# Two attentions in one kernel: algebra between them in two halves inside the loops, output per four batches inside the second loop

## The reference

```
norm_X   = layernorm(ctx, w1, b1);  norm_F = layernorm(x + tgt2, w2, b2)
attended = softmax(norm_F norm_X^T / 16) norm_X
h        = gelu(attended fc1^T + fc1_b)          # 4 values per token
cross    = h fc2^T + fc2_b                       # rank 4 plus a constant
nc       = layernorm(cross, w3, b3)
self     = softmax(nc nc^T / 16) nc
out      = norm_F + gamma2 * (cross + gamma1 * self)
```

## Time and profile before

| | us |
|---|---|
| median of 3 runs (lowest, highest) | 298.19 (297.62, 300.04) |
| the profiled execution | 298.4 |
| its span, first to last instruction | 296.5 |
| TensorE busy | 230.9 (78%) |
| VectorE busy | 203.8 (69%) |
| ScalarE busy | 138.8 (47%) |
| GpSimd busy | 115.1 (39%) |
| mean granted TensorE clock | 0.776 |
| moved by DMA | 26.79 MB, 90 GB/s mean |

### The profile page before, as it was taken

The page is one execution under the profiler, slowest core; times in us unless marked ns, Lnnn a source line. Parts: engine busy times, 40 slices in busy tenths (PEclk is TensorE's granted clock), DMA queues, the critical chain, the costliest instruction groups (busy, mean ns, idle before and its releaser), DMA issues.

```text
span 296.5 us, 4621 instructions
## 1 busy us (share of the span) xinstructions
PE 230.9 (78%) x1614; PEld 149.3 (50%) x1614; DVE 203.8 (69%) x391; ACT 138.8 (47%) x265; POOL 115.1 (39%) x141
## 2 busy tenths in 40 slices
PE   4969986199999999999999982006788888846990
PEld 4745553189888888888888850002222222212320
DVE  6586764998989888989883325994444444447991
ACT  1154572067767676767676743003533333312320
POOL 8000066979979996979972000170000000000000
PEclk9965999689999999999999999555555555555555
DMA  7940000064625262525000000000000000002997
GB/s 209 385 151 2 1 1 0 0 204 146 190 93 191 100 202 85 195 91 193 26 1 0 2 0 0 0 0 0 3 0 2 0 0 2 1 0 86 382 380 288
DMA packets 14710, 26.79 MB, mean 90 GB/s; under 512 B 1760, under 2 KB 1760, under 8 KB 14688
## 3 DMA queue, kind: packets, MB, share of 16 engines
q1 hardware_dynamic: 14688, 26.50, 25.8%
HBM read 18.11 MB, written 8.39 MB: 89 GB/s over the span
## 4 chain that ended last, share of the span: by engine, by line
PE 66%; DVE 23%; issue 4%; ACT 4%; DMA 1%; SPq 0%; DVEq 0%; ACTq 0%
PE psum L843 19%; PE psum L789 10%; DVE Fall L538 6%; PE psum L851 6%; DVE nm L493 5%; PE psum L970 5%; PE psum L812 3%; PE psum L800 3%; PE psum L940 3%; PE psum L823 3%; PE psum L881 3%; PE psum L863 3%; PE psum L759 2%; PE psum L978 1%; DVE PT L465 1%
## 5 line engine op out<-in xcount | busy, mean ns | idle before, releaser
L843 PE MATMUL psum<-XT,Fall 128*128 128x256 f32 x256 | 60.6, 379 | 0.0
L843 PEld LDWEIGHTS psum<-XT,Fall 128*128 128x128 f32 x256 | 46.1, 190 | 5.0
L575 POOL TENSOR_TENSOR xN<-xN,tgt 128x512 f32<-128x512 f32 x30 | 39.1, 1305 | 4.4 <-DVE tgt L389 2.7
L595 POOL TENSOR_SCALAR cN<-cN,nmean,rstd 128x256 f32<-128x256 f32 x64 | 36.0, 574 | 2.4 <-POOL rstd L582 2.3
L418 DVE TENSOR_REDUCE nmax<-psum 128x2 f32<-128x512 f32 x32 | 22.0, 688 | 18.7 <-PE psum L843 18.5
L692 ACT ACTIVATE PT<-psum 128x512 f32<-128x512 f32 x32 | 19.1, 597 | 33.2 <-PE psum L851 33.2
L338 DVE TENSOR_SCALAR xN<-xN,bn,rstd 128x256 f32<-128x256 f32 x64 | 29.8, 508 | 0.0
L582 POOL TENSOR_TENSOR rstd<-vps,minus_half 128x8 f32<-128x8 f32 (+1 forms) x16 | 25.3, 1580 | 9.9 <-DVE vps L329 9.7
L679 ACT ACTIVATE Fall<-psum,par 128x512 f32<-128x512 f32 x32 | 23.4, 791 | 9.2 <-PE psum L789 9.2
L698 ACT ACTIVATE E<-psum,nmax 128x256 f32<-128x256 f32 x64 | 26.6, 472 | 1.6 <-DVE nmax L418 1.6
L929 PE MATMUL psum<-identb,sU 128*128 128x128 bf16 x64 | 9.7, 306 | 19.2 <-DVE sU L273 19.2
(11 more groups left out here) (155 smaller groups left out, 369.8 us busy)
## 6 DMA issues: line engine op xcount, KB each, us to landing
cN<-ctx SPq DMA_DIRECT2D x32, 256.0 KB, 3.0
xN<-x SPq DMA_DIRECT2D x32, 256.0 KB, 4.2
out<-Fall SPq DMA_DIRECT2D x32, 256.0 KB, 3.2
x0T<-x0t SPq DMA_DIRECT2D x1, 256.0 KB, 2.7
wqT<-wqt SPq DMA_DIRECT2D x1, 256.0 KB, 3.2
c0T<-c0t SPq DMA_DIRECT2D x1, 256.0 KB, 3.8
wkT<-wkt SPq DMA_DIRECT2D x1, 256.0 KB, 4.6
wvT<-wvt SPq DMA_DIRECT2D x1, 256.0 KB, 4.9
```

What stands on the lines that cost most here:

```text
L575: pool.tensor_tensor(xN[:, b % SLOTS, :], xN[:, b % SLOTS, :], tgt2[:, :, :].rearrange("p t d -> p (t d)"), ALU.add).then_inc(y_ok, 1)
L595: pool.tensor_scalar(own, own, nmean[:, p % 4, NT * m + t:NT * m + t + 1], root_of(p, 0, m, t), ALU.add, ALU.mult)\
L843: last = pe.matmul(bank[SBANK1[b % 3]][:, t * N:(t + 1) * N], Fall[:, b, c, t * P:(t + 1) * P], XT[:, p % 4, c, m * N:(m + 1) * N], start= ...
```

## The change

- The algebra works on two groups of 32 tiles (batches 0 to 15 and 16 to 31) and is cut into six parts. Group 0's parts stand in VectorE's rounds 26 and 29 to 33 of the first loop, its GELU in ScalarE's round 28. Group 1's parts stand in steps 0 and 2 to 5 of the second loop, its GELU after the weights of step 1. GpSimd cuts group 0 before the second loop and group 1 in it.
- The products of the quadratic forms go into `kv`, the memory of the 16-head attention's keys and values, and no longer into that of `PT`.
- The transposition of the output operand (`RT`) moves from between the loops to round 30 of the first.
- The second loop has a new order on each engine. Scores have two buffers of two banks (0 to 3) in place of three; transposes of pieces and of outputs share bank 4; maxima, attended values and returns share bank 5; outputs use banks 6 and 7.
- Division and output cuts are done per quad: division on VectorE in `returned`, the cuts on GpSimd (`output_cuts`, five instructions of 8 tiles). The copy of `ha` into `co` goes to GpSimd.
- The output product comes per pair within the loop, the final addition handles two batches (1024 values per partition) per instruction, and transfers start two at a time.
- The loop has 21 steps: step `p` ends with the output of pair `p - 5`.

```diff
+GROUP = TILES // 2
+LATE = {26: (0,), 29: (1,), 30: (2,), 31: (3,), 32: (4,), 33: (5,)}
+NEXT = {0: (0,), 2: (1,), 3: (2, 3), 4: (4,), 5: (5,)}
...
-    kTm = sb("kTm", [P, 2, 2, N])
-    v1 = sb("v1", [P, NT, NH, VW])
+    kv = sb("kv", [P, 4 * N + NT * NH * VW])
+    kTm = kv[:, 0:4 * N].rearrange("p (e o n) -> p e o n", e=2, o=2)
+    v1 = kv[:, 4 * N:4 * N + NT * NH * VW].rearrange("p (t h k) -> p t h k", t=NT, h=NH)
...
-    big = PT2[:, :, :, :].rearrange("p a m n -> p (a m n)")
+    big = kv
...
     def scored(p):
-        return psum[:, 1024 * (p % 3):1024 * (p % 3 + 1)]
+        return psum[:, 1024 * (1 - p % 2):1024 * (2 - p % 2)]
+
+    def score_bank(p, m):
+        return bank[2 * (1 - p % 2) + m]
...
-            sp.wait_ge(fin_ok, b + 1)
+            sp.wait_ge(fin_ok, b // 2 + 1)
...
+        def products(v, m, n):
+
+            w = big[:, 0:GROUP * n * n].rearrange("p (t j i) -> p t j i", t=GROUP, j=n)
+            link(dve.tensor_tensor(w, v.unsqueeze(2).to_broadcast([P, GROUP, n, n]),
+                                   m.rearrange("p (j i) -> p j i", j=n).unsqueeze(1).to_broadcast([P, GROUP, n, n]),
+                                   ALU.mult))
+            return w
+
+        def newton(v, y, t):
+            link(dve.tensor_tensor(t, y, y, ALU.mult))
+            link(dve.scalar_tensor_tensor(t, t, -0.5, v, ALU.mult, ALU.mult))
+            link(dve.scalar_tensor_tensor(y, t, 1.5, y, ALU.add, ALU.mult))
+
+        def algebra(g, part):
+            G = members(g)
+            oa = OA[:, :, :, :, :].rearrange("p q t i k -> p (q t i) k")[:, G, :]
+            w5, v, y, t = W5[:, G, :], var[:, G], r3[:, G], t3[:, G]
+            if part == 0:
+                dve.wait_ge(o_saved, QUADS // 2 * (g + 1))
+                link(dve.reciprocal(rA[:, G].unsqueeze(2), oa[:, :, H:H + 1]))
+                link(dve.tensor_tensor(hpre[:, G, :], oa[:, :, 0:H], spread(rA[:, G], H), ALU.mult))
+                link(dve.tensor_tensor(hpre[:, G, :], hpre[:, G, :], c_("fc1b").unsqueeze(1).to_broadcast([P, GROUP, H]),
+                                       ALU.add), ("hpre", g))
+            elif part == 1:
+                dve.wait_ge(gelu_ok, g + 1)
+                dve.wait_ge(zero_ok, 8)
+                link(dve.tensor_reduce(w5, products(ha[:, G, :], Q[:, :], H + 1), AX.X, ALU.add))
+                link(dve.tensor_tensor(w5, w5, ha[:, G, :], ALU.mult))
+                link(dve.tensor_reduce(v, w5, AX.X, ALU.add))
+            elif part == 2:
+                link(dve.tensor_scalar(v, v, EPS, None, ALU.add))
+                link(dve.tensor_scalar(y.bitcast(I32), v.bitcast(I32), 1, None, ALU.logical_shift_right))
+                link(dve.tensor_scalar(y.bitcast(I32), y.bitcast(I32), -1.0, RSQRT_SEED, ALU.mult, ALU.add))
+                newton(v, y, t)
+            elif part == 3:
+                newton(v, y, t)
+                newton(v, y, t)
+                link(dve.tensor_tensor(u[:, G, 0:H + 1], ha[:, G, :], spread(y, H + 1), ALU.mult), ("u", g))
+            elif part == 4:
+                link(dve.tensor_reduce(uK[:, G, :], products(u[:, G, :], K[:, :], U), AX.X, ALU.add))
+            else:
+                left_cuts(uK[:, G, :], cut[:, G, 0:U], sU[:, 0, G, :], U)
+                ALG["left", g] = count[0]
...
+            for part in LATE.get(b, ()):
+                algebra(0, part)
...
         def returned(q):
+            own = slice(8 * q, 8 * (q + 1))
             dve.wait_ge(back_mm, q + 1)
-            dve.tensor_copy(OB[:, 8 * q:8 * (q + 1), :],
-                            bank[7][:, N:N + NT * P].rearrange("p (t k) -> p t k", k=VW)[:, :, 0:U]).then_inc(o2_saved, 1)
-
+            dve.tensor_copy(OB[:, own, :], bank[5][:, 0:NT * P].rearrange("p (t k) -> p t k", k=VW)[:, :, 0:U])\
+                .then_inc(o2_saved, 1)
+            dve.wait_ge(o2_saved, q + 1)
+            dve.reciprocal(rB[:, own].unsqueeze(2), OB[:, own, U - 1:U]).then_inc(h_ok, 1)
+            dve.wait_ge(h_ok, q + 1)
+            dve.tensor_tensor(co[:, own, H:CO - 1], OB[:, own, 0:H + 1], spread(rB[:, own], H + 1), ALU.mult)\
+                .then_inc(co_ok, 1)
+
+        def finish(n):
+            own = Fall[:, 2 * n:2 * n + 2, :, :].rearrange("p b c n -> p (b c n)")
+            dve.wait_ge(f_mm, n + 1)
+            dve.tensor_tensor(own, psum[:, 6 * 512:8 * 512], own, ALU.add).then_inc(fin_ok, 1)
+
+        maxima(0)
         turned(1)
-        for p in range(PAIRS + 3):
-            if p % 2 == 0 and p >= 4:
-                collected((p - 4) // 2)
-            if p % 2 == 1 and p >= 5:
-                returned((p - 5) // 2)
-            if p < PAIRS:
-                maxima(p)
-            if p % 2 == 0 and 2 <= p < PAIRS - 1:
-                turned(p + 1)
-        returned(QUADS - 1)
-
-
-        dve.wait_ge(o2_saved, QUADS)
-        ob = OB[:, :, :]
-        link(dve.reciprocal(rB[:, :].unsqueeze(2), ob[:, :, U - 1:U]))
-        link(dve.tensor_tensor(co[:, :, H:CO - 1], ob[:, :, 0:H + 1], spread(rB[:, :], H + 1), ALU.mult))
-        link(dve.tensor_copy(co[:, :, 0:H], ha[:, :, 0:H]))
-        right_cuts(co[:, :, :], cut[:, :, :], sC[:, :, :], CO)
-        ALG["sC"] = count[0]
-
-
-        for b in range(B):
-            own = Fall[:, b, :, :].rearrange("p c n -> p (c n)")
-            dve.wait_ge(f_mm, b + 1)
-            dve.tensor_tensor(own, bank[b % 4], own, ALU.add).then_inc(fin_ok, 1)
+        for p in range(2 * QUADS + 5):
+            if p + 1 < PAIRS:
+                maxima(p + 1)
+            if p % 2 == 1 and p + 2 < PAIRS:
+                turned(p + 2)
+            if p % 2 == 0 and 2 <= p < 2 * QUADS + 2:
+                collected((p - 2) // 2)
+            if p % 2 == 1 and 3 <= p < 2 * QUADS + 3:
+                returned((p - 3) // 2)
+            if p >= 5:
+                finish(p - 5)
+            for part in NEXT.get(p, ()):
+                algebra(1, part)
...
+        def right(g):
+            G = members(g)
+            to, own, left = sU[:, 1, G, :], u[:, G, :], cutR[:, G, :]
+            pool.wait_ge(alg, ALG["u", g])
+            pool.wait_ge(zero_ok, 8)
...
+        right(0)
+        for p in range(2 * QUADS + 5):
+            if p == 4:
+                right(1)
+            if p % 2 == 1 and 3 <= p < 2 * QUADS + 3:
+                output_cuts((p - 3) // 2)
...
+            if b == 28:
+                hidden(0)
+            if b == 30:
+                act.wait_ge(r_mm, 1)
+                act.activation(RT[:, :], bank[4][:, 0:DC * P // 2].bitcast(BF16), ACT.Copy).then_inc(rt_ok, 1)
...
+        for p in range(2 * QUADS + 3):
+            if p < PAIRS:
+                maxima_turned(p)
+            if p % 2 == 0 and p + 2 < PAIRS:
+                turned(p + 2)
+            if p < PAIRS:
+                weights(p)
+            if p == 1:
+                hidden(1)
+            if p % 2 == 0 and p >= 4:
+                output_turned((p - 4) // 2)
...
+        def hidden(g):
+            act.wait_ge(alg, ALG["hpre", g])
+            act.activation(ha[:, members(g), 0:H], hpre[:, members(g), :], ACT.Gelu).then_inc(gelu_ok, 1)
...
         def turn(p):
             if p >= 1:
                 pe.wait_ge(sT_ok[(p - 1) % 2], (p + 1) // 2)
-            if p >= 3:
-                pe.wait_ge(m_ok, p - 1)
+            if p >= 7 and p % 2 == 1:
+                pe.wait_ge(cT_ok, (p - 5) // 2)
+            if p == QUADS:
+                pe.wait_ge(alg, ALG["left", 1])
+                pe.wait_ge(right_ok, 12)
...
         def maxima_turn(p):
             pe.wait_ge(max2_ok, p + 1)
-            k = min(max(p + 1, 2), PAIRS - 1)
-            pe.wait_ge(sT_ok[k % 2], k // 2 + 1)
-            pe.wait_ge(sT_ok[(k - 1) % 2], (k - 1) // 2 + 1)
-            pe.transpose(bank[6][0:2 * VW, NT * P:NT * P + P // 2].bitcast(BF16), nm2[:, p % 2, :, :].rearrange("p m r -> p (m r)"),
+            if p >= 3 and p % 2 == 1:
+                pe.wait_ge(o2T_ok, (p - 1) // 2)
+            if p >= 4 and p % 2 == 0:
+                pe.wait_ge(o2_saved, (p - 2) // 2)
...
+        def output_turn(q):
+            pe.wait_ge(sC_ok, 5 * q + 5)
+            k = min(2 * q + 6, PAIRS - 1)
+            pe.wait_ge(sT_ok[k % 2], k // 2 + 1)
+            for half in range(2):
+                for t in range(NT):
+                    k = (half * NT + t) * P // 2
+                    last = pe.transpose(bank[4][:, k:k + P // 2].bitcast(BF16), couple(sC, q, t, half), identb[:, :])
+            last.then_inc(ct_mm, 1)
...
         def scores(p):
             pe.wait_ge(sT_ok[p % 2], p // 2 + 1)
-            if p >= 3:
-                pe.wait_ge(exp2_ok, p - 2)
+            if p >= 2:
+                pe.wait_ge(exp2_ok, p - 1)
...
+        def output(n):
+            pe.wait_ge(cT_ok, n // 2 + 1)
+            if n >= 1:
+                pe.wait_ge(fin_ok, n)
+            for c in range(DC):
+                for m in range(2):
+                    rows = slice(SLOT * m, SLOT * m + SC)
```

(84 more changed lines are left out.)

117 lines of the change are left out of this document (26 added, 91 removed).

## The result

The changed kernel takes 268.04 us (median of 4 runs, 267.74 to 268.70), the kernel before 298.09 beside it: ratio 0.9003, 95% interval 0.8965 to 0.9041. Forecast were 272.0, range 263 to 280. The profiled execution is one of 268.7 with a span of 266.9, so 1.8 lies around it.

A forecast was written before the change was run, and what follows sets the result against it. Bare on the path: 19.1 us of algebra, 7.0 of cuts and lead-in, 25.5 of output. First transposes at 183.8 plus 86.6 to the end give a 270.4 span; with 1.9 around it, 272 us, range 263 to 280.

The forecast's parts named there:

- First half hidden but for parts 4 and 5: End of first loop: only parts 4 and 5 don't fit; first transposes at 183.8 for 200.04, 16.2 us gained.
- Startup, steps 0 to 6: Start of second loop: VectorE also carries the second half's 11.45 us; step 7 starts about 36.0 us after the first transposes.
- A pair at the half clock: Second loop, from step 7: an even and an odd step on TensorE cost 7.74 us, taken as 7.85.
- The clock: Second loop: TensorE stays at 0.50; the rival, chance 0.14, has full clock back and 264 us.
- Steps 7 to 15: Second loop after the startup: 33.3 us at 7.85 a pair, including small waits, to 69.3 from the first transposes.
- the small products: Second loop: the new loop keeps the old one's small products, an argument against the clock's return; no time given.
- Maxima transposes that wait for VectorE: Second loop: such waits in most steps were named as a sign of being wrong; no size given.
- Tail: After step 15: last outputs alternate with additions on one pair of banks; 13 us, to 82.3 from the first transposes.
- Last transfers: After the last addition: two transfers of 256 KB, 4.3 us with both issues, for 6.2 before.
- VectorE and GpSimd in each other's way: Second loop: GpSimd's cuts beside VectorE cost 8 us more, 280; chance 0.10. The forecast itself took near zero.
- Serial: Second loop: each step becomes one chain, a pair costs 13.9 us, total 305, slower than before; chance 0.04.
- not doing what it says: Both loops: parts wait on the other group so that nothing overlaps, and the time doesn't change; chance 0.02.

The follow-up runs named there:

- the extra matmuls: The changed kernel with extra, unused 128x128 by 128-column matmuls on TensorE in the gap between the loops and where TensorE waits in the second loop: 260.5 us, ratio 0.8738.
- two extra matmuls: The changed kernel with 2 extra matmuls each before the maxima transposes of steps 8, 10, 12 and 14 alone: 266.9 us, ratio 0.8940.

## Why the prediction was right, and where not

Span 270.4 was forecast and 266.9 measured. By the steps of the sum:

- *First half hidden but for parts 4 and 5.* First transposes at 183.8 forecast, 185.07 measured. The first loop's first maximum came 1.0 later than before (64.32 for 63.36), which no edit explains: the clock comes up 1.1 us later in the first stage. 0.3 is left. The `oTq` copy behind part 5 was at 184.3 for 183.0. 0.4 of that is what I had put at nothing: two of part 5's cuts took 0.54 and 0.61 us beside GpSimd's, where two rounds earlier, with GpSimd idle, they took 0.36 each. The last eight maxima took 25.4 us for 24.7; of these 0.7, the scores that wait for the last evacuation behind the GELU make 0.4, for the 0.5 taken. Right.
- *Startup, steps 0 to 6.* 36.0 forecast, 35.44 measured, with each wait where it was put: `collected(0)` behind ScalarE's second GELU, `turn(8)` behind part 5 (the 2.3 in the list of waits). Leaving the second half out took 6.9 us off these steps. Right.
- *A pair at the half clock.* 7.85 forecast, 7.81 measured. Right.
- *The clock.* Forecast 0.50 throughout, with 0.14 for its return. This is the step that failed, in size, and a full clock in the loop was among the signs that I had named for being wrong. After the pair at 220.51 to 228.32 it rose, and fell again in each even step from step 10 on. The measured 268.0 lies midway between the forecast and this rival's 264. Steps 7 to 15 took 30.1 in place of 33.3, which is nearly the whole miss. The profiles of the six other kernels with the output in the loop and no extra matmuls there show it come back too; with the output after the loop TensorE is busy 6.26 of 7.29, and the clock is never above 0.50. When it comes differs between executions: in the second one of the changed kernel TensorE is busy for 10.00 of 10.00 us from 233 to 243, all at 0.50, and only then the clock is up again. I had seen that the new loop lies between stages that rose and stages that didn't, and gave the precedent of the small products too much weight. The rival's own time, 264, was for the full clock throughout; only the extra matmuls came to that, and to less.
- *Maxima transposes that wait for VectorE.* Such waits in most steps were another sign of being wrong that I had named. They came in all of steps 0 to 6, where VectorE was forecast as the limit from step 2 on, and in three of steps 7 to 15, 0.7 us each, at the full clock. In the pair at the half clock they didn't wait.
- *Tail.* 13.0 forecast, 13.2 measured; the single buffer's 2.02 a pair is taken away by the second pair of banks.
- *Last transfers.* 4.3 forecast, 3.1 measured: landing without a backlog is 2.3 us in the profile after, for 3.2 in the earlier trace rows.
- *VectorE and GpSimd in each other's way.* All 16 additions take 1.22 us, and the five cuts 1.5 us a pair; the zero that I took was right for them. It can be seen on VectorE's other instructions: part 5's cuts above, and small links of 0.37 and 0.34 for 0.19, beside the cuts at 204.5 to 205.3.
- *Serial, and not doing what it says.* Neither: a pair stayed far below 12.6, and undoing either half of the change costs 14 us. (The terms listed for the serial case add up to 5.6 for the odd step and not 5.9, which makes it 303 and not 305.)

The Trainium skill (TensorE: Matmul & The Clock Gate, "Part 1: The HAM clock gate") has sustained activity release the throttle. Here the traces agree only in part. The clock did rise out of stretches in which TensorE didn't idle, but their lengths differ widely, as the stretches before the first rise show, in the changed kernel, with group 0 two rounds earlier, and with part 1 ahead of `collected(0)`:

```profile
216.55:229.20 12.65, 12.65 (x95) 4.52 (x96) 8.25 (x12) 6.16 (x10) 1.49 (x5) 0.50 0.28 103
...
216.20:235.60 19.40, 19.40 (x144) 6.85 (x145) 13.11 (x21) 9.66 (x16) 2.99 (x10) 0.50 0.31 112
...
212.70:217.00 4.30, 4.30 (x35) 1.58 (x37) 1.81 (x3) 2.17 (x4) 0.00 (x0) 0.50 0.15 55
```

And in the last of these runs, 19.00 us without idle time (228 to 247) brought no rise at all.

What stays open: why the clock came back after 4, 13 or 19 us without idle time in nearly the same sequence of instructions, and once not at all; why the spells at full clock end in the changed kernel after three to four microseconds and not with two extra matmuls; and why the clock comes back sooner in some first stages than in others. The last is behind most of the 1 to 3 us by which single executions differ up to the first transposes.
